# One-hot destination matrices made by comparing broadcast destination numbers instead of transposing, and a three-part pick done as one matrix product

## The chip, the cores and the metric

The kernel runs on one core of one Trainium2 chip. The metric is the device time of one execution in microseconds (us); a comparison of two kernels is by the median of several executions of each.

## What is computed

Eight blocks work one after the other on a matrix `x` of 1875 nodes by 256 features; each adds its result to `x`. Four are graph layers over the same 31,875 edges, which are sorted by destination (`dst`). The change touches two of the eight: it writes a table during the second block, and reads it in the third, the relational attention. The third block computes

```python
h_all = jnp.einsum('nf,rof->rno', x, W).reshape(r, n, h, d)      # r = 8 relations, h = 8 heads, d = 32
h_src, h_dst = h_all[edge_type, src], h_all[edge_type, dst]
scores = jnp.einsum('ehd,hd->eh', h_src, attn_src) + jnp.einsum('ehd,hd->eh', h_dst, attn_dst)
...                                                             # leaky relu, softmax over the edges of a destination
out = jax.ops.segment_sum(h_src * w[..., None], dst, num_segments=n)
```

and the second block lets the better half of the nodes, by a router weight, through a feed-forward network:

```python
weights = (jnp.einsum('bsd,do->bso', x, wr) + br)[..., 0]
_, idx = jax.lax.top_k(weights, k)
processed = jnp.zeros_like(x).at[batch_idx, idx[:, :kk]].set(y)  # y: the network's rows, times the weight
```

## The kernel before

**Tiling.** Nodes stand in T = 15 tiles of P = 128. Edges stand in EC = 264 chunks of 128, a chunk's edges all having their destination in one node tile; `g.dst[:, c]` holds for chunk c, one edge per partition, the destination's number within its tile (0 to 127), and a register `tiles[u]` says which tile. `g.dst`, `g.etype` and a large SBUF buffer `g.attrs_t` of [128, 264, 128] bf16 (the trace calls it `edge_space`) live through the whole program. Each phase (`Phase`) writes one program per engine by hand, with semaphores between them; the engines meet at a phase's end.

**The stage that the change rewrites** is `relation_rows` (phase `score`, 2376 to 2701 us in the profiled execution). It does two things side by side, in 22 passes of U = 12 chunks, each of 3 groups of G = 4 chunks.

- It makes the table `h_table` in DRAM, one node tile a pass in the first 15 passes ("product passes" below; the other 7 have none): ScalarE copies the tile of x to `x_tile` (L1965), TensorE makes four units of two relations each (`products`, L1924, two units before the picks and two behind them, in two PSUM buffers `p_rows`), ScalarE copies them to `rows` (L1974, L1977), and SyncE writes `rows`, 1,056 KB, to DRAM (L1898). `rows` is a single buffer: L1974 waits until the write has landed.
- It picks, for each edge, the destination's 64 attention numbers (8 relations x 8 heads) out of `score_dst`, by a product with a matrix that has a 1 where the edge's destination stands. VectorE compares `g.dst` with a row of numbers, once per chunk (`hot`, L1997), TensorE transposes the result (L1935), ScalarE copies it out of PSUM into `g.attrs_t` (L1969), and TensorE multiplies it by the numbers, which are held as three bf16 parts `parts[:, tile, k, :]` that sum to the f32 value: three matmuls of 64 columns per chunk, added up in PSUM (L1945). VectorE multiplies the sum by a 0/1 mask of the edge's relation (`rel`, made by L1991; L2004) and adds over the relations (L2008).

Beside these, GpSimd sends the scatters of a later block's adjacency matrix (`g.adj.send`, an indirect DMA of 128 values each, L488): two per group, once the group's comparisons are done (`hot_ready`), 132 in the stage. They are also sent in other phases, 45 of them in `rank`.

**The phases in the second block.** `rank_tokens` (phase `rank`, L1053 to L1109) computes a weight per node (L1080), writes the weights to DRAM and loads them back onto every partition (L1063, semaphore `w_spread`), and then counts with VectorE, in a loop over 15 tiles, how many nodes have a larger one (L1097 and its like). The DMA queue of ScalarE has nothing in it. `scatter_tokens` (phase `spread`) then sends the 15 tiles of rows with GpSimd (L1271) to their places; VectorE has nothing to do in it.

Of the kernel before, what the change touches and what calls it, by code (L numbers as in the profile page):

```python
# [13 lines left out]
P = 128  # L14
# [1025 lines left out]
def rank_tokens(nc, g, xn, wr, br, chosen, r):  # L1040
# [4 lines left out]
    with Phase(nc, "rank") as ph:  # L1045
# [5 lines left out]
        p_turned = ph.ps("p_turned", [T, P])  # L1051
        loaded, w_ready, w_turned, w_copied = (ph.sem(s) for s in ("loaded", "w_ready", "w_turned", "w_copied"))
# [16 lines left out]
        @block.tensor  # L1069
        def _(pe):  # L1070
            pe.wait_ge(w_ready, 1)
            nc.tensor.transpose(p_turned[:, :], w[:, :], g.ident[:, :]).then_inc(w_turned, 1)

# [187 lines left out]
def scatter_tokens(nc, g, rows, r, slots):  # L1261

    with Phase(nc, "spread") as ph:
# [4 lines left out]
        def _(pool):  # L1268
# [4 lines left out]
            pool.wait_ge(sent, 16 * r.choices * T)  # L1273

# [216 lines left out]
def capacity_ffn(nc, g, i):  # L1491

    chosen = max(max(1, int(0.5 * N)) - 1, 1)
    with Phase(nc, "cap") as ph:
# [7 lines left out]
        scatter_tokens(nc, g, xn, r, slots)  # L1502
# [359 lines left out]
def relation_rows(nc, g, score_src, score_dst, scores, xt, wt, h_table):  # L1862
# [4 lines left out]
    with Phase(nc, "score") as ph:  # L1867
        hot = ph.sb("hot", [P, U, P], BF16)
# [7 lines left out]
        rel, picked = ph.sb("rel", [P, U, R]), ph.sb("picked", [P, U, R, HD])  # L1876
        groups = U // G
        p_hot = [ph.ps(f"p_hot{b}", [P, G, P], BF16) for b in range(groups)]
        p_dst = [ph.ps(f"p_dst{b}", [P, G, 2 * S]) for b in range(groups)]
        turn, hot_ready, turned, copied = (ph.sem(x) for x in ("turn", "hot_ready", "turned", "copied"))  # L1880
# [4 lines left out]
        def _(sp):  # L1885

            sp.sem_inc(turned, groups)
            sp.sem_inc(copied, groups)
# [14 lines left out]
        def _(pool):  # L1903
            nc.gpsimd.iota(rel_idx[:, :], [[1, R]], base=0, channel_multiplier=0,
                           allow_small_or_imprecise_dtypes=True).then_inc(iota_made, 1)
            for n in range(EC // G):
                pool.wait_ge(hot_ready, n + 1)
                g.adj.send(pool, 2)

        @block.tensor  # L1910
        def _(pe):
# [47 lines left out]
        def _(act):  # L1959
# [21 lines left out]
            with act.Fori(T, EC // U) as i:  # L1981
                one_pass(i, False)
# [510 lines left out]
```

## Time and profile before

| what | value |
|---|---|
| median of 3 executions | 4655.58 us (4652.52 to 4660.18) |
| the profiled execution | 4685.71 us, its span 4684.1 us |
| busy over the span: TensorE, VectorE, GpSimd, ScalarE | 62%, 47%, 40%, 19% |
| `relation_rows` (phase `score`) | 2376 to 2701 us |
| its 15 product passes, its 7 others | 2387 to about 2613, to 2701 us |
| `rank` after the weights are back, until its end | 2119.1 to 2163.4 us |
| `spread` of the second block: first and last send | 2166.3, 2184.2 us |

The busy shares are means over eight blocks with different limits; what the change is worth is to be read in the stages it touches. The span is from the first to the last recorded instruction; the profiled execution is 30.1 us longer than the median of the three others.

### The profile page before, as it was taken

The numbers are of one execution on the slowest core, as the hardware profiler recorded it, in microseconds if no ns is written. First come the engines' busy times: TensorE is split into PE (matmuls) and PEld (weight loads), VectorE is DVE, ScalarE is ACT, GpSimd is POOL, SyncE is SP. The second block draws the span as 40 slices with busy tenths as digits, with TensorE's granted clock in tenths as the row PEclk, the third lists the DMA queues.
The fourth block names the chain that finished last, engine by engine and source line by source line (L and its number), as shares of the span: only waits on it lengthen the run. The fifth ranks groups of instructions, "written<-read, shape, count | busy, mean of one in ns | idle before, by whom it ended". The sixth has DMA issues, their size and how long they took to land. (4 is left out here: it accounts for less than half of the span.)

```text
span 4684.1 us, 57224 instructions
## 1 busy us (share of the span) xinstructions
PE 2923.7 (62%) x16851; PEld 2401.0 (51%) x16852; DVE 2212.2 (47%) x5663; ACT 867.9 (19%) x2228; POOL 1871.3 (40%) x1982
## 2 busy tenths in 40 slices
PE   3566746664666566642568626665949639947392
PEld 3455535553555355522556413335938639936382
DVE  6655645554555555564243437681064421134113
ACT  1122312221222122210112100001300103310020
POOL 4366546664666466624323467731010020020212
PEclk7788878777887778875678657676979859978696
DMA  6633323332333233303312133315947449945594
GB/s 157 217 89 89 78 65 89 88 83 59 89 90 88 57 87 89 89 15 124 100 55 74 28 82 93 92 41 190 304 145 240 150 159 328 325 150 174 181 333 128
DMA packets 357397, 598.97 MB, mean 128 GB/s; under 512 B 81862, under 2 KB 239864, under 8 KB 354808
## 3 DMA queue, kind: packets, MB, share of 16 engines
q1 hardware_dynamic: 245816, 357.76, 23.3%
q0 software_dynamic: 88640, 214.25, 16.3%
q10 hardware_dynamic: 22656, 23.54, 1.5%
q8 instruction: 132, 2.16, 0.2%
q14 instruction: 153, 1.25, 0.1%
HBM read 499.63 MB, written 95.75 MB: 127 GB/s over the span
## 5 line engine op out<-in xcount | busy, mean ns | idle before, releaser
L833 POOL DMA_INDIRECT gine_got<-gine_table,src x1056 | 1024.5, 970 | 619.7 <-issue 251.1
L893 PE MATMUL gine_p_sum<-gine_hot,gine_got 128*128 128x128 f32 x4224 | 846.2, 334 | 565.1 <-DVE stack_acc L930 200.1
L893 PEld LDWEIGHTS gine_p_sum<-gine_hot,gine_got 128*128 128x128 f32 x4224 | 707.4, 238 | 719.0 <-issue 648.6
L922 DVE TENSOR_TENSOR gine_got<-gine_got,gine_p_edge 128x256 f32<-128x256 f32 x1056 | 440.2, 418 | 633.5 <-PE gine_p_edge L884 365.0
L901 ACT ACTIVATE gine_got<-gine_got 128x256 f32<-128x256 f32 x1056 | 439.0, 417 | 1201.1 <-issue 750.5
L488 POOL DMA_INDIRECT adjacency<-value,place x264 | 281.1, 1065 | 475.9 <-POOLq L54 166.2
L930 DVE TENSOR_TENSOR stack_acc<-stack_acc,gine_p_sum 128x256 f32 x1056 | 438.9, 416 | 3.5 <-issue 0.7
L883 PE MATMUL gine_p_edge<-gine_w_a,edge_space 128*128 128x256 bf16 x1056 | 338.3, 320 | 42.6 <-issue 34.7
L1368 PE MATMUL ffn_p_h<-ffn_xt,ffn_w 128*128 128x128 f32 x2864 | 347.3, 279 | 1.1 <-DMA ffn_w<-in_L_ffn_w 0.7
L1368 PEld LDWEIGHTS ffn_p_h<-ffn_xt,ffn_w 128*128 128x128 f32 x2864 | 337.3, 196 | 3.8 <-DMA ffn_w<-in_L_ffn_w 2.6
L884 PE MATMUL gine_p_edge<-gine_w_b,edge_space 128*128 128x256 bf16 x1056 | 336.8, 319 | 0.0
L1380 PE MATMUL ffn_p_y<-ffn_w,ffn_ht 128*128 128x256 f32 x1432 | 328.8, 380 | 4.7 <-DMA ffn_w<-in_L_ffn_w 3.9
L2224 POOL DMA_INDIRECT edge_space<-h_table,hrow x264 | 273.8, 1037 | 123.0 <-issue 74.6
L2259 PE MATMUL inorder_p_sum<-edge_space,inorder_hot 128*128 128x265 f32 x528 | 230.9, 553 | 145.2 <-DVE edge_space L2332 95.9
L1434 DVE TENSOR_TENSOR ffn_y<-ffn_p_y,ffn_b 128x256 f32<-128x256 f32 x112 | 47.6, 425 | 549.4 <-PE ffn_p_y L1380 549.4
L1405 ACT ACTIVATE ffn_ht<-ffn_p_h,ffn_b 128x128 f32<-128x128 f32 x716 | 204.8, 368 | 548.3 <-PE ffn_p_h L1368 548.3
L1633 PE MATMUL gcn_p_out<-gcn_h,gcn_a 128*128 128x256 f32 x1350 | 298.7, 379 | 0.0
L1380 PEld LDWEIGHTS ffn_p_y<-ffn_w,ffn_ht 128*128 128x128 f32 x1432 | 263.6, 190 | 38.3 <-DMA ffn_w<-in_L_ffn_w 6.7
L1633 PEld LDWEIGHTS gcn_p_out<-gcn_h,gcn_a 128*128 128x128 f32 x1350 | 253.8, 190 | 32.9
L2259 PEld LDWEIGHTS inorder_p_sum<-edge_space,inorder_hot 128*128 128x128 f32 x528 | 110.8, 252 | 236.6 <-issue 230.0
L1146 POOL IOTA route_e_idx<- 128x8 f32 (+1 forms) x3 | 0.4, 135 | 570.2 <-POOLq L54 570.2
L844 DVE TENSOR_TENSOR gine_hot<-iota_free,dst 128x512 f32<-128x512 f32 x264 | 182.6, 692 | 66.1 <-PE gine_p_sum L893 33.0
(398 smaller groups left out, 3526.2 us busy)
## 6 DMA issues: line engine op xcount, KB each, us to landing
gcn_a<-adjacency SPq DMA_DIRECT2D x270, 320.0 KB
ffn_w<-in_L_ffn_W SPq DMA_DIRECT2D x74, 1024.0 KB
ffn_w<-in_L_ffn_w SPq DMA_DIRECT2D x60, 1024.0 KB
ffn_w<-in_L_ffn_w SPq DMA_DIRECT2D x90, 512.0 KB
adjacency<-zero_row ACTq DMA_DIRECT2D x3, 7200.0 KB, 43.8
gine_got<-gine_table,src POOLq DMA_INDIRECT x1056
h_table<-score_rows SPq DMA_DIRECT2D x15, 1056.0 KB
adjacency<-zero_row SPq DMA_DIRECT2D x1, 7200.0 KB, 28.1
```

The lines of the kernel that those rows point to most:

```text
L488: pool.indirect_dma_start(self.tables[c % 2], bass.IndirectOffsetOnAxis(ap=self.place[:, c:c + 1], axis=0), self.value[:, c:c + 1], None). ...
L833: pool.indirect_dma_start(got[:, c % RING, :], None, table, bass.IndirectOffsetOnAxis(ap=rows[:, c:c + 1], axis=0)).then_inc(gathered[c % ...
L883: nc.tensor.matmul(p_edge[c % 4][:, 0:D], g.attrs_t[:, c, :], w_a[:, :], start=True, stop=False)
L884: nc.tensor.matmul(p_edge[c % 4][:, 0:D], g.attrs_t[:, c, :], w_b[:, :], start=False, stop=True).then_inc(edge_done, 1)
L893: ins = nc.tensor.matmul(p_sum[d % 4][:, half * P:(half + 1) * P], got[:, d % RING, half * P:(half + 1) * P], hot[:, d % HOTS, :], start=T ...
L901: nc.scalar.activation(got[:, c % RING, :], got[:, c % RING, :], ACT.Relu).then_inc(msg_ready, 1)
L922: nc.vector.tensor_tensor(got[:, c % RING, :], got[:, c % RING, :], p_edge[c % 4][:, 0:D], ALU.add).then_inc(summed, 1)
L930: nc.vector.tensor_tensor(a, a, p_sum[d % 4][:, 0:D], ALU.add).then_inc(added, 1)
L1368: ins = nc.tensor.matmul(p_h[n % 2][m // 4][:, m % 4, :], w1_sb[:, n % 2, k, m * P:(m + 1) * P], xt[:, n % 2, k, :], start=(k == 0), stop= ...
L1380: ins = nc.tensor.matmul(p_y[n % 2][:, 0:D], ht[:, n % 2, m, :], w2_sb[:, n % 2, m, :], start=(m == 0), stop=(m == m_all - 1))
L1633: ins = nc.tensor.matmul(p_out[d][:, 0:D], a[:, n % RA, d * P:(d + 1) * P], h[:, t, :], start=(t == 0), stop=(t == T - 1))
L2259: nc.tensor.matmul(p_sum[c % SUMS][:, 0:WIDE], hot[:, c % HOTS, :], got[:, c % HELD, :], start=True, stop=True).then_inc(agg_done, 1)
```

## The change

A table of the destination numbers is made once, in `rank_tokens`: TensorE transposes `g.dst` (three pieces of 88 chunks), ScalarE copies them as bf16 and writes them to DRAM (`dst_lines`), and, once `w_spread` has come, issues three DMAs that bring the whole list onto every partition of `g.attrs_t` (3 x 128 x 22,528 bytes, 2.88 MB each). In `scatter_tokens` VectorE compares the buffer with the partition's own number, in place, in three instructions of 11,264 columns: that gives the turned 0/1 matrices of all 264 chunks. `relation_rows` loses the comparisons, the transposes and the copies; TensorE multiplies each chunk by all three parts at once (one matmul of 192 columns), and VectorE adds the three parts up, from PSUM, before it multiplies by the mask. GpSimd's two scatters per group now wait for the group's picks (`dst_done`).

```diff
@@ rank_tokens
+        K = 3
+        lines, lane_rows = g.dram("dst_lines", [EC * P], BF16), ph.sb("lane_rows", [EC // K, K, P], BF16)
+            for k in range(K):
+                ins = nc.tensor.transpose(p_lanes[:, k, :], g.dst[:, k * (EC // K):(k + 1) * (EC // K)], g.ident[:, :])
+            ins.then_inc(lanes_turned, 1)
             pe.wait_ge(w_ready, 1)
...
+        @block.scalar
+        def _(act):
+            act.wait_ge(lanes_turned, 1)
+            nc.scalar.copy(lane_rows[:, :, :], p_lanes[:, :, :]).then_inc(lanes_copied, 1)
+            act.wait_ge(lanes_copied, 1)
+            act.dma_start(lines.rearrange("(k c e) -> c k e", k=K, e=P), lane_rows[:, :, :]).then_inc(lanes_written, 16)
+            act.wait_ge(lanes_written, 16)
+            act.wait_ge(w_spread, 16)
+            for k in range(K):
+                some = slice(k * (EC // K), (k + 1) * (EC // K))
+                act.dma_start(g.attrs_t[:, some, :].rearrange("p c e -> p (c e)"), row(lines[some.start * P:some.stop * P]))\
+                    .then_inc(g.lanes_in, 16)
@@ scatter_tokens
+        @block.vector
+        def _(v):
+            if not mark_lanes:
+                return
+            v.wait_ge(g.lanes_in, 48)
+            for k in range(0, EC, EC // 3):
+                some = g.attrs_t[:, k:k + EC // 3, :]
+                nc.vector.tensor_scalar(some, some, g.iota_part[:, 0:1], None, ALU.is_equal)
@@ relation_rows
-        hot = ph.sb("hot", [P, U, P], BF16)
-        p_hot = [ph.ps(f"p_hot{b}", [P, G, P], BF16) for b in range(groups)]
-        p_dst = [ph.ps(f"p_dst{b}", [P, G, 2 * S]) for b in range(groups)]
+        p_dst = ph.ps("p_dst", [P, U // 2, 512])
...
             for n in range(EC // G):
-                pool.wait_ge(hot_ready, n + 1)
+                pool.wait_ge(dst_done, n + 1)
                 g.adj.send(pool, 2)
...
-                for b in range(groups):
-                    pe.wait_ge(hot_ready, i * groups + (b + 1))
-                    pe.wait_ge(copied, i * groups + (b + 1))
-                    for u in range(b * G, (b + 1) * G):
-                        ins = nc.tensor.transpose(p_hot[b][:, u % G, :], hot[:, u, :], g.ident_b[:, :])
-                    ins.then_inc(turned, 1)
...
                     pe.wait_ge(picked_done, i * groups + (b + 1))
-                    pe.wait_ge(copied, i * groups + (b + 1 + groups))
                     for u in range(b * G, (b + 1) * G):
-                        for k in range(3):
-                            ins = nc.tensor.matmul(p_dst[b][:, u % G, 0:S],
-                                                   g.attrs_t[:, bass.ds(i * U + u, 1), :].rearrange("p a e -> p (a e)"),
-                                                   parts[:, bass.ds(tiles[u], 1), k, :].rearrange("p a s -> p (a s)"),
-                                                   start=(k == 0), stop=(k == 2))
+                        ins = nc.tensor.matmul(p_dst[:, u // 2, u % 2 * 3 * S:(u % 2 + 1) * 3 * S],
+                                               g.attrs_t[:, bass.ds(i * U + u, 1), :].rearrange("p a e -> p (a e)"),
+                                               parts[:, bass.ds(tiles[u], 1), :, :].rearrange("p a k s -> p (a k s)"),
+                                               start=True, stop=True)
...
-                for b in range(groups):
-                    act.wait_ge(turned, i * groups + (b + 1 + groups))
-                    act.sem_inc(turn, 1)
-                    nc.scalar.copy(g.attrs_t[:, bass.ds(i * U + b * G, G), :], p_hot[b][:, :, :]).then_inc(copied, 1)
...
-                    v.wait_ge(turned, i * groups + (b + 1))
-                    for u in range(b * G, (b + 1) * G):
-                        ins = nc.vector.tensor_scalar(hot[:, u, :], g.iota_free[:, :], g.dst[:, bass.ds(i * U + u, 1)], None,
-                                                      ALU.is_equal)
-                    ins.then_inc(hot_ready, 1)
-                for b in range(groups):
...
                     v.wait_ge(dst_done, i * groups + (b + 1))
-                    nc.vector.tensor_tensor(picked[:, some, :, :], p_dst[b][:, :, 0:S].rearrange("p u (r h) -> p u r h", r=R),
-                                            rel[:, some, :].unsqueeze(3).to_broadcast([P, G, R, HD]),
-                                            ALU.mult).then_inc(picked_done, 1)
+                    nc.vector.tensor_reduce(summed[:, some, :].rearrange("p (a u) s -> p a u s", u=2),
+                                            p_dst[:, banks, 0:6 * S].rearrange("p a (u k s) -> p a u s k", u=2, k=3),
+                                            AX.X, ALU.add).then_inc(picked_done, 1)
+                    v.drain()
+                    nc.vector.tensor_tensor(picked[:, some, :, :], summed[:, some, :].rearrange("p u (r h) -> p u r h", r=R),
+                                            rel[:, some, :].unsqueeze(3).to_broadcast([P, G, R, HD]), ALU.mult)
                     v.drain()
                     nc.vector.tensor_reduce(scores[:, bass.ds(i * U + b * G, G), :], picked[:, some, :, :].rearrange("p u r h -> p u h r"),
                                             AX.X, ALU.add)
```

On TensorE the body of a product pass began before as follows (`ISA` and `REGISTER_ALU` rows are address arithmetic; the last row shown stands 36 times in a pass, each with an `ISA`):

```order
L793 ISA x2
L1935 MATMUL score_p_hot<-ident_b,score_hot 128x128 x4
...
L1931 REGISTER_ALU
L1935 MATMUL score_p_hot<-ident_b,score_hot 128x128 x4
L1919 REGISTER_ALU
L1921 ISA
L1924 MATMUL score_p_rows<-score_wt,score_x_tile 128x256 x4
L1921 REGISTER_ALU
L1924 MATMUL score_p_rows<-score_wt,score_x_tile 128x256 x4
L1942 REGISTER_ALU
L1945 ISA
L1945 MATMUL score_p_dst<-score_parts,edge_space 128x64
```

The same place now:

```order
L793 ISA x2
L1947 ISA
L1950 MATMUL score_p_rows<-score_wt,score_x_tile 128x256 x4
L1947 REGISTER_ALU
L1950 MATMUL score_p_rows<-score_wt,score_x_tile 128x256 x4
L1960 ISA
L1962 ISA
L1962 MATMUL score_p_dst<-score_parts,edge_space 128x192
```

The products are now the first thing in a pass, and the last row shown stands 12 times in a pass.

On VectorE a group's work stood after all 12 comparisons of its pass:

```order
L1997 TENSOR_SCALAR score_hot<-iota_free,dst 128x128
L1997 ISA
L1997 TENSOR_SCALAR score_hot<-iota_free,dst 128x128
L2004 TENSOR_TENSOR score_picked<-score_p_dst,score_rel 128x256
L2008 ISA
L2008 TENSOR_REDUCE rgat_scores<-score_picked 128x32
```

The same place now, with the first rows of the pass:

```order
L2002 TENSOR_TENSOR score_rel<-score_rel_idx,etype 128x96
L2007 ISA
L2008 TENSOR_REDUCE score_summed<-score_p_dst 128x256
L2012 TENSOR_TENSOR score_picked<-score_summed,score_rel 128x256
L2015 ISA
L2015 TENSOR_REDUCE rgat_scores<-score_picked 128x32
```

The comparisons are gone; each group has three instructions in place of two, and of them only the first reads PSUM. The multiplication L2012 now has both operands in SBUF.

## Rows read from the trace of the kernel before

**Rows 1.** Windows: awaiting `rank_every`, product passes, other passes.

```profile
core 0: us, PE busy (x) PEld busy (x) DVE busy (x) ACT busy (x) POOL busy (x), PEclk, DMA share, GB/s
2114.90:2119.20 4.30, 0.00 (x0) 0.00 (x0) 0.07 (x2) 0.00 (x0) 3.38 (x4) 0.50 0.67 229
2387.00:2613.00 226.00, 199.83 (x1206) 157.39 (x1207) 86.57 (x285) 63.21 (x134) 86.42 (x90) 0.84 0.25 67
2613.00:2701.00 88.00, 50.96 (x334) 32.31 (x331) 37.64 (x120) 12.54 (x22) 38.73 (x40) 0.53 0.04 13
```

**Rows 2.** Timeline of VectorE: starts of passes 2, 16 and 22.

```profile
2399.36 0.26 DVE L1991 TENSOR_TENSOR score_rel<-score_rel_idx,etype 128x96 f32<-128x96 f32 x1 [0.47 <-issue]
...
2609.24 0.26 DVE L1991 TENSOR_TENSOR score_rel<-score_rel_idx,etype 128x96 f32<-128x96 f32 x1 [0.45 <-issue]
...
2688.35 0.26 DVE L1991 TENSOR_TENSOR score_rel<-score_rel_idx,etype 128x96 f32<-128x96 f32 x1 [0.45 <-issue]
```

**Rows 3.** Timeline (start, us, engine ... [idle before <-releaser]), product pass.

```profile
2567.27 0.33 SPq L1898 DMA_DIRECT2D h_table<-score_rows  x1
2567.48 3.72 PE L1924 MATMUL score_p_rows<-score_wt,score_x_tile 128*128 128x256 f32 x16
...
2571.03 1.05 PE L1945 MATMUL score_p_dst<-score_parts,edge_space 128*128 x20
2572.04 0.24 ACT L1974 COPY score_rows<-rgat_in_score_src 128x64 f32 x1 [3.24 <-DMA h_table<-score_rows]
2572.23 0.97 POOL L488 DMA_INDIRECT adjacency<-value,place  x1 [0.30 <-issue]
...
2574.73 0.42 DVE L2004 TENSOR_TENSOR score_picked<-score_p_dst,score_rel 128x256 f32<-128x256 f32 x1 [7.58 <-PE score_p_dst L1945]
```

**Rows 4.** Timeline, the next product pass: `h_table` write, its landing.

```profile
2583.32 0.33 SPq L1898 DMA_DIRECT2D h_table<-score_rows  x1
...
2592.29 0.24 ACT L1974 COPY score_rows<-rgat_in_score_src 128x64 f32 x1 [7.43 <-DMA h_table<-score_rows]
```

**Rows 5.** Timeline of a pass without products.

```profile
2639.81 3.69 PE L1945 MATMUL score_p_dst<-score_parts,edge_space 128*128 x22
...
2644.43 0.96 POOL L488 DMA_INDIRECT adjacency<-value,place  x1 [0.30 <-issue]
...
2645.25 0.42 DVE L2004 TENSOR_TENSOR score_picked<-score_p_dst,score_rel 128x256 f32<-128x256 f32 x1 [5.89 <-PE score_p_dst L1945]
```

**Rows 6.** VectorE by line and shape: busy us, mean ns | idle before.

```profile
L2008 DVE TENSOR_REDUCE rgat_scores<-score_picked 128x256 f32 x66 | 40.4, 612 | 12.1 <-issue 12.1
L586 DVE TENSOR_REDUCE pairs_total<-pairs_p_sum 128x88 f32<-128x264 f32 x3 | 1.3, 426 | 0.0
L2004 DVE TENSOR_TENSOR score_picked<-score_p_dst,score_rel 128x256 f32<-128x256 f32 x66 | 28.0, 425 | 170.3 <-PE score_p_dst L1945 109.0 <-DMA unpack_rows<-in_edge_rows 59.3
```

**Rows 7.** The same view: a cast and a copy to bf16.

```profile
L440 DVE CAST unpack_parts<-unpack_rows 128x768 bf16<-128x768 f32 x11 | 6.2, 563 | 18.5 <-DMA unpack_rows<-in_edge_rows 18.5
L910 DVE COPY gine_w_a<-gine_parts 32x256 bf16<-32x256 bf16 x16 | 4.1, 257 | 0.5
```

**Rows 8.** Timeline of `rank`: a VectorE operation and a send.

```profile
2103.17 4.16 DVE L1080 TENSOR_TENSOR rank_prod<-cap_xn,rank_wr 128x3840 f32<-128x3840 f32 x1 [2.63 <-DMA rank_br<-in_L_ffn_br]
2103.28 4.90 POOL L488 DMA_INDIRECT adjacency<-value,place  x1 [0.30 <-issue]
```

**Rows 9.** Instructions of L1271: duration min/median/max, first and last start.

```profile
L1271 POOL DMA_INDIRECT cap_slots<-cap_xn,cap_slot x15: 965/971/973, 2166.3 to 2184.2; - x15
```

**Rows 10.** Timeline of `rank`: weights' load, ranking's first and last instruction.

```profile
2114.58 0.33 SPq L1063 DMA_DIRECT2D rank_every<-router_weights  x1
...
2119.13 2.21 DVE L1097 TENSOR_SCALAR_CACHE_REDUCE rank_junk<-rank_every,rank_w 128x1920 f32<-128x1920 f32 x1 [6.05 <-issue]
...
2163.21 0.17 DVE L1109 SCALAR_TENSOR_TENSOR cap_gate<-rank_rank,rank_w 128x15 f32<-128x15 f32 x1
```

More of the change, by code:

```diff
@@ L1051, in rank_tokens @@
         p_turned = ph.ps("p_turned", [T, P])
+        K = 3
+        lines, lane_rows = g.dram("dst_lines", [EC * P], BF16), ph.sb("lane_rows", [EC // K, K, P], BF16)
+        p_lanes = ph.ps("p_lanes", [EC // K, K, P])
+        lanes_turned, lanes_copied, lanes_written = (ph.sem(s) for s in ("lanes_turned", "lanes_copied", "lanes_written"))
         loaded, w_ready, w_turned, w_copied = (ph.sem(s) for s in ("loaded", "w_ready", "w_turned", "w_copied"))
@@ L1258, in _, with scatter_tokens @@
             nc.vector.tensor_scalar(r.expert[:, :], owner[:, :], float(ne - 1), None, ALU.min)
-def scatter_tokens(nc, g, rows, r, slots):
+def scatter_tokens(nc, g, rows, r, slots, mark_lanes=False):
     with Phase(nc, "spread") as ph:
@@ L1501, in capacity_ffn @@
         rank_tokens(nc, g, xn, i["L0_ffn_wr"].rearrange("d o -> (d o)"), i["L0_ffn_br"], chosen, r)
-        scatter_tokens(nc, g, xn, r, slots)
+        scatter_tokens(nc, g, xn, r, slots, mark_lanes=True)
         expert_blocks(nc, g, slots, results, r, i["L0_ffn_w1"].rearrange("(a d) f -> a d f", a=1), i["L0_ffn_b1"],
@@ L1875, in relation_rows @@
         rel_idx = ph.sb("rel_idx", [P, R])
-        rel, picked = ph.sb("rel", [P, U, R]), ph.sb("picked", [P, U, R, HD])
+        rel, picked, summed = ph.sb("rel", [P, U, R]), ph.sb("picked", [P, U, R, HD]), ph.sb("summed", [P, U, S])
         groups = U // G
-        p_hot = [ph.ps(f"p_hot{b}", [P, G, P], BF16) for b in range(groups)]
-        p_dst = [ph.ps(f"p_dst{b}", [P, G, 2 * S]) for b in range(groups)]
-        turn, hot_ready, turned, copied = (ph.sem(x) for x in ("turn", "hot_ready", "turned", "copied"))
+        p_dst = ph.ps("p_dst", [P, U // 2, 512])
+        turn = ph.sem("turn")
         split, dst_done, picked_done, iota_made = (ph.sem(x) for x in ("split", "dst_done", "picked_done", "iota_made"))
@@ L1885, in _ @@
         def _(sp):
-            sp.sem_inc(turned, groups)
-            sp.sem_inc(copied, groups)
             sp.sem_inc(picked_done, groups)
@@ L1980, in _ @@
                 one_pass(i, True)
-            with act.Fori(T, EC // U) as i:
-                one_pass(i, False)
         @block.vector
@@ L1993, in _ @@
                 for b in range(groups):
-                    v.wait_ge(turned, i * groups + (b + 1))
-                    for u in range(b * G, (b + 1) * G):
-                        ins = nc.vector.tensor_scalar(hot[:, u, :], g.iota_free[:, :], g.dst[:, bass.ds(i * U + u, 1)], None,
-                                                      ALU.is_equal)
-                    ins.then_inc(hot_ready, 1)
-                for b in range(groups):
-                    some = slice(b * G, (b + 1) * G)
-                    v.wait_ge(dst_done, i * groups + (b + 1))
-                    nc.vector.tensor_tensor(picked[:, some, :, :], p_dst[b][:, :, 0:S].rearrange("p u (r h) -> p u r h", r=R),
-                                            rel[:, some, :].unsqueeze(3).to_broadcast([P, G, R, HD]),
-                                            ALU.mult).then_inc(picked_done, 1)
+                    some, banks = slice(b * G, (b + 1) * G), slice(b * G // 2, (b + 1) * G // 2)
+                    v.wait_ge(dst_done, i * groups + (b + 1))
+                    nc.vector.tensor_reduce(summed[:, some, :].rearrange("p (a u) s -> p a u s", u=2),
[4 more added lines that the diff above has]
+                                            rel[:, some, :].unsqueeze(3).to_broadcast([P, G, R, HD]), ALU.mult)
                     v.drain()
@@ L2009, in _ @@
                                             AX.X, ALU.add)
-                    v.drain()
+                v.drain()
 def edge_scores(nc, g, h_table, scores):
@@ L2452, in build @@
         g.tile_of = sb("tile_of", [P, EC])
+        g.lanes_in = nc.alloc_semaphore("lanes_in")
         g.adj = Adjacency(nc, g, sb)
```

## The prediction

> **What bounds the kernel now.** I read the windows first, because the change lives in three places only: `rank` and `spread` of the second block, and the stage `relation_rows`. In the 15 product passes TensorE is busy 199.8 of 226 us, at a mean granted clock of 0.84; in the other passes 51.0 of 88 us, at 0.53, with VectorE at 37.6 us and GpSimd at 38.7 us [rows 1]. So no engine is full, and a busy share does not say what a pass costs. The starts of passes do: (2609.24 - 2399.36)/14 = 14.99 us for a product pass, (2688.35 - 2609.24)/6 = 13.19 us for another [rows 2]. All of the stage that the change can reach is 15 x 14.99 + 7 x 13.19 = 317 us.
>
> The timeline then shows what ends the waits in a product pass [rows 3]. Two halves of products cost 3.72 us each. The first group's 12 picks are over some 0.6 us after 2571.03 (20 take 1.05 us), but VectorE begins only at 2574.73, 1.53 us after the last of GpSimd's six sends ends (2572.23 + 0.97 = 2573.20). The pass without products shows it again: a third of 36 picks at 22 in 3.69 us would be done by 2641.8, and VectorE begins at 2645.25, in the last send [rows 5]. TensorE's finished work seems to be held while the sends run; the trace does not say why, and the sixth send is what I count from. The second limit is the table: written from 2567.27, landed at 2572.04, 4.8 us [rows 3]; the next takes 9.0 us (2583.32 to 2592.29) [rows 4]. Four passes of 15 have such a long one, the rest 4.3 to 5.0 us.
>
> **The change part by part.**
>
> *The stage, by its limits.* TensorE in a product pass: 1.06 us between passes, 3.72 + 3.72 for products, and 12 picks of 192 columns. One of 64 columns costs 1.05/20 = 0.052 us [rows 3], so between 12 x 0.052 = 0.6 us if width were free and three times that, 1.9; taken near the upper, 1.5. Sum 10.0.
>
> The table chain: the write 5.0 us, then ScalarE's copies 0.95, two units 3.72, a last copy 0.6: 10.3 us, and with the long write of rows 4 14.5; the mean over 11 and 4 is 11.4. The change takes nothing from this chain but the copies that stood beside it.
>
> VectorE: a group costs the new reduction R, then 0.425 for the product, 0.18 between, 0.61 for the second reduction and 0.24 of drains, 1.45 together [rows 6]; a pass has three groups and 0.8 for the mask. R adds 768 numbers up to 256 from PSUM, an operation that the trace lacks in this size. L586 (264 numbers from PSUM) takes 0.426; with a fixed 0.15 (L1109 takes 0.17 for 15 numbers [rows 10]) that is 1.05 ns per number, R = 0.95. L2008 takes 0.612 for 256 numbers read with a stride, 1.80 ns per number, R = 1.53. If L2008's extra 0.185 us is a price per output (32 outputs, 5.8 ns each), 256 outputs add 1.48 to 0.95: R = 2.43. The new one strides through its input as L2008 does, so I take 1.53: 3 x (1.53 + 1.45) + 0.8 = 9.7 us a pass, with 8.0 and 12.4 as ends. The picks wait for R of the group before in time (`picked_done`), and TensorE's other work hides that.
>
> GpSimd: six sends at 0.97 + 0.30 [rows 3] are 7.6 us, and now wait for the picks rather than for the comparisons. Behind each pair nothing is queued but the next pair; who suffers is the holding above. If it goes on, the last send ends 1.06 + 3.72 + 0.5 + 7.6 = 12.9 us after a pass's start, and with 1.5 a pass is 14.4 us. If it does not, the table's 11.4 stands. The hold is there in most product passes of the trace, so two parts to one: 13.4 us. **15 x (14.99 - 13.4) = 24 us saved.** In the other passes VectorE's 9.7 is the limit, plus some waiting on sends: 10.5. **7 x (13.19 - 10.5) = 19 us saved.** What the comparisons, transposes and ScalarE's copies cost lies in those passes already and is not counted again.
>
> *`rank`.* Transposes, a copy and a 68 KB write fit before `w_spread` (2119.1). Then 3 x 2.88 = 8.65 MB go onto 128 partitions. The load of `rank_every` moved 229 GB/s [rows 1], which makes 38 us; they land by 2119.1 + 38 = 2157, before VectorE's ranking ends at 2163.2 [rows 10]. Nothing else is on ScalarE's queue, and VectorE waits for `lanes_in` after the ranking only. Cost 0; without that cover up to 38 us.
>
> *`spread`.* Three comparisons of 11,264 columns in place, beside 15 sends from 2166.3 on [rows 9]. L910's 0.257 us for 256 bf16 numbers, less the fixed 0.15, is 0.42 ns each: 4.9 us a comparison. L440's 0.563 for 768 (from f32) gives 0.54 ns and 6.2 us [rows 7]. Beside a 4.16 us VectorE operation a send took 4.90 us in place of 0.97 [rows 8]: sends stand still while such an operation runs. Fully held the phase grows by 3 x 4.9 = 14 to 18 us; not at all, if sends slip between, 0. The first may start before a send is out, so I take 10.
>
> The Trainium skill (page "SBUF — State Buffer", section "SBUF: two separate sides") says that a VectorE operation in a two-port mode, or with two SBUF inputs against a GpSimd operation that reads SBUF, holds the port pair that the two share, and that GpSimd can then write no descriptors; the trace agrees with 4.90 beside 4.16 us [rows 8]. The page "VectorE: DVE Perf Modes" (section "The perf-mode tier table (the rule you actually need)") gives 693 ns for 2048 bf16 columns of such an operation; an estimate from it is 3.1 us a comparison, 9 us for three, and the sum would be better by 1 us or so.
>
> *Sum.* -24 - 19 + 10 = -33 us on the profiled 4685.7. That execution is 30 us over the median of 4655.6, and part of the holds may be due to its recording, so I take 10 off: -23, 4633 us.
>
> **The rivals.**
>
> *R1, the forecast*, chance 0.41: held in part, 4633, own range 4605 to 4655.
>
> *R2, the holds vanish*, 0.18. The sends now start in step with VectorE's reduction and are spread over a pass; for it speaks that the hold was seen where six sends ran in a row, against it that six in a row still follow the first picks, if picks are quick. Passes 11.4 and 9.7: -54 - 24 + 10 = -68, 4588 us.
>
> *R3, the reduction is dear*, 0.17. R = 2.43 makes VectorE's pass 12.4. For it: 256 outputs of three inputs each, which L2008 (eight each) and L586 price differently [rows 6]. Product passes 13.9, others 12.8: -16 - 3 + 10 = -9, 4647 us.
>
> *R4, slower: the new product waits on the sends*, 0.12. L2012 has both operands in SBUF, L2004 had one in PSUM, and the send released by the same `dst_done` reads SBUF just then. If each group's product waits for one send (0.97 us) and R is 2.43, VectorE's pass is 12.4 + 3 = 15.4: 15 x 0.4 + 7 x 2.2 + 10 = +31, 4687 us. It decides once VectorE's pass is over 15.0 us, and in the seven others from 13.2. Rows 8 show the block in the other direction; no row shows a VectorE operation waiting for a send. The skill's rule above would let whichever starts first block the other, which is this rival.
>
> *R5, the change does not do what it says*, 0.12: product passes stay at 15.0, set by hold and table write, and the others gain 0.7: -5 + 10 = +5, 4661 us.
>
> **How the numbers follow.** The time is R1's. From 4582 to 4668 lie R1, R3, R5 and most of R2; outside are R4 and the low tail of R2, 2 in 10 together. A measurement of this kernel tells about 0.2% (9.3 us) from no change. Faster by more than that: R1 but 0.05, R2, and half of R3, 0.63; slower: R4 and 0.04 of R5, 0.16; within: the rest, 0.21.
>
> **What would show it right or wrong.** Pass starts (now at L2002) 13.4 us apart with products, 10.5 without; L2008 at 1.5 us (0.95 and 2.4 are the others' values); L2012 at 0.43 or, by R4, over 1 us; L2008 idle before it "PE score_p_dst" long after the picks' end, if the hold stays; the last broadcast landed before 2163, and the sends of `spread` ending near 2195 in place of 2185. The prediction falls if `lanes_in` comes after the ranking, if other phases move by more than 5 us, or if the comparisons take over 7 us each.

## The result, and the profile after

The median went from 4655.0 us (4652.5 to 4660.2) to 4587.7 us (4581.3 to 4589.7), a ratio of 0.9851 with an interval of 0.9837 to 0.9866: 67 us faster, three times the forecast of 23 us and within 1 us of what the rival "the holds vanish" gave. One execution of e9_all_moved, 5759 us where its three others took 4304 to 4308, is left out of all times below.

The starts of passes 2, 16 and 22 in the changed kernel's timeline of VectorE:

```profile
2384.97 0.26 DVE L2002 TENSOR_TENSOR score_rel<-score_rel_idx,etype 128x96 f32<-128x96 f32 x1 [0.47 <-issue]
...
2539.46 0.26 DVE L2002 TENSOR_TENSOR score_rel<-score_rel_idx,etype 128x96 f32<-128x96 f32 x1 [0.45 <-issue]
...
2589.08 0.26 DVE L2002 TENSOR_TENSOR score_rel<-score_rel_idx,etype 128x96 f32<-128x96 f32 x1 [0.45 <-issue]
```

A product pass takes (2539.46 - 2384.97)/14 = 11.03 us where it took 14.99, another pass (2589.08 - 2539.46)/6 = 8.27 where it took 13.19 [rows 2]. That is 14 x 3.96 + 6 x 4.92 = 85 us of the profiled execution; the whole stage is 88 us shorter. The same two stretches as windows:

```profile
core 0: us, PE busy (x) PEld busy (x) DVE busy (x) ACT busy (x) POOL busy (x), PEclk, DMA share, GB/s
2384.97:2539.46 154.49, 122.77 (x605) 100.52 (x604) 84.84 (x141) 36.78 (x82) 81.28 (x85) 0.94 0.35 95
2539.46:2589.08 49.62, 21.02 (x87) 8.96 (x85) 36.07 (x60) 0.58 (x1) 33.41 (x35) 0.57 0.07 22
```

GpSimd's sends fill 81 us of 154 now, and VectorE 36 of 50 in the other passes. The granted clock rose from 0.84 in the product passes [rows 1] to 0.94. VectorE's instructions by line and shape (busy, mean ns):

```profile
L2008 DVE TENSOR_REDUCE score_summed<-score_p_dst 128x256 f32<-128x768 f32 x66 | 62.7, 950 | 71.4 <-PE score_p_dst L1962 68.8 <-issue 2.6
L2012 DVE TENSOR_TENSOR score_picked<-score_summed,score_rel 128x256 f32<-128x256 f32 x66 | 28.2, 427 | 6.1
```

The new reduction takes 0.95 us, the lower of the three values in the prediction, and the multiplication with two SBUF operands 0.427, as before with one in PSUM [rows 6]. All 66 of these lie between 0.424 and 0.478 us: none waits for a send of 0.97. A product pass in the timeline of all engines:

```profile
2412.65 1.15 PE L1962 MATMUL score_p_dst<-score_parts,edge_space 128*128 x12
2412.94 0.24 ACT L1987 COPY score_rows<-rgat_in_score_src 128x64 f32 x1 [3.98 <-DMA h_table<-score_rows]
...
2413.18 0.96 DVE L2008 TENSOR_REDUCE score_summed<-score_p_dst 128x256 f32<-128x768 f32 x1 [9.24 <-PE score_p_dst L1962]
2413.42 0.97 POOL L488 DMA_INDIRECT adjacency<-value,place  x1 [9.20 <-PE score_p_dst L1962]
...
2413.72 3.72 PE L1950 MATMUL score_p_rows<-score_wt,score_x_tile 128*128 128x256 f32 x16
...
2415.76 0.58 ACT L1990 COPY score_rows<-score_p_rows 128x512 f32<-128x512 f32 x1 [1.60 <-issue]
...
2417.48 0.58 ACT L1990 COPY score_rows<-score_p_rows 128x512 f32<-128x512 f32 x1 [1.14 <-PE score_p_rows L1950]
```

The reduction starts 0.5 us after the first pick, and the two copies 2.04 and 3.76 us after the products' start, while six sends run from 2413.42 on. These copies wait for products whose own records end 1.86 and 3.72 us after that start, so nothing holds them. Before, VectorE stood until 1.5 us behind the sixth [rows 3]. The hold on which the forecast counted is gone from the product passes, although the six sends still follow each other without a break there.

It, or something like it, remains elsewhere. Of the six other passes four take 7.2 us, one 8.8 and one 11.9. In the last of these TensorE's picks come 2.8 us apart, and VectorE stands until 3 us after the last of six sends (which ended at 2561.50):

```profile
2563.45 0.32 PE L1962 MATMUL score_p_dst<-score_parts,edge_space 128*128 x1 [2.47 <-issue]
...
2564.68 0.96 DVE L2008 TENSOR_REDUCE score_summed<-score_p_dst 128x256 f32<-128x768 f32 x1 [4.56 <-PE score_p_dst L1962]
```

That one pass is 0.8 us of the mean of 8.27.

Product passes are not alike either: of three, two take 9.2 to 9.5 us and one 13.9 to 16.6. In the long one the table write is long (timeline; its landing is what L1987 waits for):

```profile
2427.77 0.70 SPq L1924 DMA_DIRECT2D h_table<-score_rows  x1
...
2435.25 0.24 ACT L1987 COPY score_rows<-rgat_in_score_src 128x64 f32 x1 [7.41 <-DMA h_table<-score_rows]
```

7.5 us from issue to landing, 4.0 in the short passes (2408.90 to 2412.94).

What the change costs lies in `spread`. The comparisons as instructions of their line, and the first row send beside them in the timeline:

```profile
L1303 DVE TENSOR_SCALAR edge_space<-edge_space,iota_part x3: 3149/3149/3155, 2143.7 to 2149.9; 128x11264 bf16<-128x11264 bf16 x3
...
2144.34 5.73 POOL L1292 DMA_INDIRECT cap_slots<-cap_xn,cap_slot  x1 [4.62 <-PEq L54]
```

Three times 3.15 us. The first row send takes 5.73 us and the second 3.48, where one takes 0.97 [rows 9]. From the first to the last of the 15 it is now 25.1 us where it was 17.9 [rows 9]: 7.2 us lost, all in these two. `rank` is unchanged, 63.2 us from its multiplication to the first row send before and 63.3 now. The three transfers have landed some 20 us before the ranking ends. In a later profile (e15) they take 23.9 us, from 1890.0 to 1913.9, in place of the 38 of the prediction.

In the profiles the two kernels differ by 104 us, in the medians by 67. Some 22 us of that lie ahead of `rank` (its multiplication at 2103.2 and 2081.0), where the kernels are the same; four more profiles at that speed have 2082 to 2086, so the profiled execution of before was long there. The rest, 82 us, is 15 us more than the medians show.

### The profile page after: what moved, and what is told of

It reads as the page before. It is cut to its first block and busy times, and to the rows that moved or that the text cites. A ratio compares the mean times of both kernels' runs of the same rounds, so it can differ in the third digit from the quotient of the medians.

```text
span 4579.6 us, 54274 instructions
## 1 busy us (share of the span) xinstructions
PE 2819.1 (62%) x16062; PEld 2325.5 (51%) x16063; DVE 2228.5 (49%) x5468; ACT 832.3 (18%) x2163; POOL 1874.5 (41%) x1982
```

## The experiments

"Product pass" and "other" are the means over passes 2 to 15 and 16 to 21, from the starts of the instruction that makes the mask `rel`, as above. The chips differ: e1 to e4 ran on one (chip 10) where the kernel before takes 4654 us, the others on three (chips 0, 3 and 9) where it takes 4363 to 4367, most of the difference ahead of `rank`. The first comparison's chip is not on record; its kernel before took 4655 us, as on chip 10. "The slower chip" below is that of the 4654 and 4655 us. Each row has the time of the kernel before beside it, and ratios are to that. Runs with "no_sends", and e16, leave out half of the adjacency matrix's entries, so their result is incomplete.

| run | before, us | ratio (interval) | product pass | other |
|---|---|---|---|---|
| before / changed | 4655 | 1 / 0.985 (0.984 to 0.987) | 14.99 / 11.03 | 13.19 / 8.27 |
| e1_gate | 4654 | 1.003 (1.002 to 1.005) | 14.84 | 11.57 |
| e2_one_pick | 4654 | 1.007 (1.005 to 1.009) | 17.31 | 11.58 |
| e3_three_picks | 4654 | 1.001 (1.000 to 1.002) | 16.22 | 9.19 |
| e4_before_no_sends | 4654 | 0.989 (0.988 to 0.991) | 12.54 | 11.23 |
| e5_after_no_sends | 4365 | 0.981 (0.978 to 0.984) | 9.40 | 7.21 |
| e6_after_unrolled | 4365 | 0.989 (0.986 to 0.992) | 11.13 | 7.81 |
| e7_three_picks_no_sends | 4365 | 0.992 (0.989 to 0.995) | 12.30 | 8.12 |
| e8_sends_moved | 4365 | 0.989 (0.986 to 0.991) | 9.41 | 7.21 |
| e9_all_moved | 4367 | 0.986 (0.984 to 0.988) | 9.41 | 7.21 |
| e10_marks_moved | 4367 | 0.988 (0.986 to 0.990) | 10.89 | 7.28 |
| e11_pick_thrice | 4367 | 0.992 (0.990 to 0.994) | 11.69 | 7.24 |
| e12_thrice_no_sends | 4367 | 0.987 (0.986 to 0.989) | 11.23 | 7.23 |
| e13_narrow_apart | 4367 | 0.993 (0.992 to 0.995) | 12.30 | 7.89 |
| e14_wide_addresses | 4367 | 0.991 (0.990 to 0.993) | 11.72 | 7.23 |
| e15_after_again | 4367 | 0.989 (0.987 to 0.991) | 10.98 | 7.30 |
| e16_memset_for_sends | 4367 | 0.992 (0.990 to 0.995) | 12.54 | 8.09 |
| e17_before_again | 4363 | 1.001 (0.999 to 1.003) | 13.23 | 10.92 |
| e18_three_picks_again | 4363 | 0.996 (0.994 to 0.997) | 12.55 | 8.11 |

### One part of the change at a time

**e1_gate**: only the semaphore of the sends.

```diff
-                pool.wait_ge(hot_ready, n + 1)
+                pool.wait_ge(dst_done, n + 1)
```

> The kernel before with one line changed: GpSimd's two sends per group wait for the group's picks (dst_done) instead of its comparisons. Theories. A, many picks: TensorE's 36 picks of 64 columns per pass, each with address arithmetic, are what makes a product pass 15.0 us; B, sends: six sends in a row beside the first products hold TensorE's finished work; C, round trip: comparison, transpose, copy and pick stand one behind the other. By B product passes fall to about 11.5 us and the time to about 4600 us; by A and C it stays within 10 us of 4655, or is a little slower since the sends start later (up to 4680).

Product passes stayed at 14.8 us and the time rose by 0.3%, so theory B (the sends) failed in the form in which it was put. But the hold had only moved. From its timeline, in a stretch at full granted clock (1.00 from 2473.3 to 2488.0):

```profile
2480.79 3.71 PE L1924 MATMUL score_p_rows<-score_wt,score_x_tile 128*128 128x256 f32 x16
...
2484.67 1.02 POOL L488 DMA_INDIRECT adjacency<-value,place  x1 [0.30 <-issue]
2485.47 0.58 ACT L1977 COPY score_rows<-score_p_rows 128x512 f32<-128x512 f32 x1 [6.43 <-issue]
...
2487.03 0.58 ACT L1977 COPY score_rows<-score_p_rows 128x512 f32<-128x512 f32 x1 [0.98 <-DMA unpack_rows<-in_edge_rows]
```

The picks, now ahead of the sends, reach VectorE at once; the products behind them do not reach ScalarE at 2482.7 and 2484.5, as their records would have it, but at 2485.5 and 2487.0, the second 1.3 us behind the last send. In the passes without products nothing is left to hold, and they fell to 11.6.

**e2_one_pick**: only the picks; comparisons, transposes and copies stay.

```diff
-                        for k in range(3):
-                            ... p_dst[b][:, u % G, 0:S], ..., parts[:, bass.ds(tiles[u], 1), k, :] ...
+                        ... p_dst[:, b % 2 * 2 + u % G // 2, ...], ..., parts[:, bass.ds(tiles[u], 1), :, :] ...
```

> The kernel before with the second part of the change alone: one product of 192 columns per chunk and the sum of three parts on VectorE; comparisons, transposes and copies stay. The transposes share two PSUM buffers in place of three, and the picks two in place of three. By A (many picks) product passes fall to 11.5 to 12.5 us, the others to 11, time about 4605; by C (round trip) and B (sends) it stays at 4645 to 4665, since VectorE has 3 x 0.53 us more to do.

Slower by 0.7%, which no theory had. All product passes but the first last 17.3 us, to within 0.2. TensorE waits 3.9 us in each for a picks' buffer that two groups share. The hold is there too: the first reading begins 1.2 to 1.4 us after the last of the six sends in each of the passes 2 to 15. In one of them:

```profile
2513.01 0.97 POOL L488 DMA_INDIRECT adjacency<-value,place  x1 [0.31 <-issue]
...
2515.18 0.96 DVE L2005 TENSOR_REDUCE score_picked<-score_p_dst 128x256 f32<-128x768 f32 x1 [7.26 <-DMA unpack_rows<-in_edge_rows]
```

The eight picks before it ended at 2512.66 by their records, and the granted clock was 1.00 from 2506.0 to 2517.5, so a halved clock is not what holds them. (The DMA that the row names as releaser, `unpack_rows`, was over some 2000 us before.) Passes 2 to 6 have 6.8 us at half clock and the later ones 3.4, and they last the same 17.3 us. So one wide pick is no gain without the rest; how much of the loss is the hold and how much the fewer buffers this run does not say.

**e3_three_picks**: the changed kernel with the old picks and the old reading of them.

```diff
-                        ins = nc.tensor.matmul(p_dst[:, u // 2, u % 2 * 3 * S:(u % 2 + 1) * 3 * S], ..., parts[..., :, :], start=True, stop=True)
+                        for k in range(3):
+                            ins = nc.tensor.matmul(p_dst[b][:, u % G, 0:S], ..., parts[..., k, :], start=(k == 0), stop=(k == 2))
```

> The changed kernel with the old picks: three products of 64 columns per chunk, summed in PSUM, on the ready matrices. By A (many picks) product passes go back to 14 us or more and the time to about 4635; by C (round trip) it stays at 4580 to 4595; by B (sends gated by the picks) the same as C.

This speaks for theory A, the many picks: with the matrices ready but 36 narrow picks the whole gain was gone, 16.2 us a product pass. So on this chip neither half of the change is worth anything by itself.

**e4_before_no_sends**: `g.adj.send` left out of the stage.

> The kernel before without the 132 scatters of the stage (the adjacency matrix lacks half of its entries). By B (sends hold TensorE's results) product passes fall to about 11.5 us and the others to 10: about 4595 us. By A or C alone they stay at 15.0 and 13.2: 4655 us, less what the sends cost elsewhere.

12.5 us in place of 15.0, and 11.2 in place of 13.2: 1.1% faster, 47 us, where theory B alone had 11.5, 10 and 59. The sends cost the kernel before that much, and the forecast had rightly read that they do. The product passes are of two kinds: six of 11.6 us, at a granted clock of 0.92 to 1.00, and eight of 13.2 to 13.3, at 0.89 to 0.91.

### The sends and the table write in the changed kernel

**e5_after_no_sends**: the same edit in the changed kernel.

> The changed kernel without the 132 scatters of the stage (the adjacency matrix lacks half of its entries). In its profile two of three product passes last 9.4 us and the third 14 to 16, since the table write takes 8 us in place of 4. Theory S, sends and quick writes together make the long writes: all product passes 9.4 us or so, 15 x 1.6 = 24 us less, about 4563 us, all writes 3.5 to 4 us. Theory W, the write itself stalls when the stage writes quickly: the long writes stay, within 8 us of 4587.

Theory S (sends and quick writes together make the long writes) held: every product pass 9.4 us, from 9.2 to 9.5, every table write as short as the short ones, the granted clock 1.00. Against the changed kernel on such a chip (e15, 4319 us) it is 31 us less, where 24 were expected. The window of its product passes:

```profile
2173.43:2305.09 131.66, 116.78 (x621) 96.57 (x619) 84.93 (x140) 37.36 (x83) 0.00 (x0) 1.00 0.27 115
```

9.4 is TensorE's own chain (1.06 + 3.72 + 1.15 + 3.72 = 9.65, less the overlap of picks and products), 7.2 VectorE's: 3 x (0.95 + 0.43 + 0.61 + 0.18) + 0.7.

**e8_sends_moved** sent them in the next block's feed-forward phase, seven per block of rows:

```diff
+                if ne == 8 and affine is None and g.adj.next < EC:
+                    g.adj.send(pool, 7)
                 pool.wait_ge(y_ready, n + 1)
```

> The changed kernel with the 132 scatters sent in the feed-forward phase of the next block, seven behind each other per block of rows, in place of this stage. If the holds come from their neighbourhood in this stage and GpSimd has room in the later phase, the time is that of the run without sends, about 4565 us; if they hold the later phase's results (7 x 1.27 = 9 us per block of some 10), up to 4600 us.

The stage did fall to 9.4 and 7.2, and the time stayed at that of the changed kernel: the other phase went from 148.2 to 172.6 us for its 22 results, 8.2 us a block, since 7 x 1.27 = 8.9 us of sends are more than the 7.06 that a block took. The expectation had "some 10" for the 7.06, which was not read from a row.

**e10_marks_moved** put the comparisons, in twelve pieces, beside the capacity network's matrix work, where VectorE waits.

```diff
+                if mark_lanes and n < 6:
+                    if n == 0:
+                        v.wait_ge(g.lanes_in, 48)
+                    for k in range(2 * n * 22, (2 * n + 2) * 22, 22):
+                        some = g.attrs_t[:, k:k + 22, :]
+                        nc.vector.tensor_scalar(some, some, g.iota_part[:, 0:1], None, ALU.is_equal)
```

> The changed kernel with the comparisons alone moved, in twelve pieces, beside the capacity network's matrix work. If their 9.3 us hold GpSimd's row sends in spread, as the trace says (25.2 us from the first to the last in place of 17.9), the time falls by 7 us; if the phase is set by something else, it stays. The stage itself stays at 11.0 and 8.3 us per pass.

`spread` went back to 17.8 us, and the median was 4310 against 4319 of the changed kernel, on chips with the same time for the kernel before: 9 us, with intervals that overlap.

**e9_all_moved** has both, with three and five sends per block.

> The changed kernel with both costs moved to where their engine waits: the comparisons of the table in twelve pieces beside the capacity network's matrix work (VectorE waits there), and all 132 scatters out of the stage: three per block of rows in the capacity network (24) and five per block in the next block's (108), since seven per block, 8.9 us, were over that phase's 7.06 us per block. Expected: the stage 204 us in place of 236, the sends of spread 18 us in place of 25, the two networks unchanged: 35 us under the changed kernel. If the sends slow the networks' TensorE by being beside it, half of that is lost.

The fastest version that computes everything: 4304 us, 0.986 of the kernel before against 0.989. The stage takes 204 us in place of 228 (e15), but the next block's network 164.5 in place of 148.2 though five sends (6.4 us) fit into its 7.06 us, so 16 of 24 us were paid back: worse than the expectation's second case. (Both versions with moved sends change a wait in a branch for edge orders that don't occur here; it would need care.)

### Whose hold is it

**e6_after_unrolled**:

```diff
-            with pe.Fori(0, T) as i:
+            with pe.Fori(0, T // 2) as j:
+                one_pass(2 * j, True)
+                one_pass(2 * j + 1, True)
+            with pe.Fori(T - 1, T) as i:
                 one_pass(i, True)
```

> The changed kernel with TensorE's loop over product passes unrolled by two: the same instructions executed, twice as many in the loop's body (about 260 in place of 130). Theory H1, a long loop body is what delays TensorE's results beside GpSimd's sends (the kernel before had some 250 in a body): product passes go up by 2 to 4 us, time 4615 to 4640. Theory H2, the length of the body is without effect, and the number of instructions executed in a pass counts: 4583 to 4592.

Theory H2: 11.13 us against 10.98 for the changed kernel on such a chip (e15), no effect.

**e7_three_picks_no_sends** closes the square.

> Three picks per chunk on the ready matrices, as in the run with three picks, and without the stage's 132 scatters. With one pick per chunk against three (12 and 36 per pass) and with and without sends this makes a square of four. If the sends are what makes 36 picks dear, this falls from 4664 to about 4590 us, and product passes from 16.2 to 11.5; if the picks are dear by themselves, it stays above 4640.

12.3 us. With three picks the sends would cost 3.9 us a pass (16.2 to 12.3), with one 1.6 (11.0 to 9.4). That looked settled, but the four corners of the square were not on one chip.

**e11_pick_thrice** and **e12_thrice_no_sends** (`for _ in range(3):` around the wide pick):

> The changed kernel with every pick issued three times over (36 products of 192 columns per pass, the same result), with the sends. Theory I: 36 picks with their weight loads and address arithmetic are what lets GpSimd's sends hold back TensorE's next products, whatever their width: the copies of the second half's products come 2.5 us late or more, product passes go to 15.5 to 17 us, time about 4670 on the chip of 4655 (ratio 1.00). Theory P: the old shape, 64 columns summed in PSUM, did it: the passes grow by TensorE's own work alone, 24 x 0.08 = 1.9 us and 0.1 us of issue each, to some 13.5 us.

> The same without the stage's 132 scatters (the adjacency matrix lacks half of its entries). By theory I product passes fall to about 12.5 us; the difference to the run with sends is then 3 us or more per product pass, against 1.6 with twelve picks. By theory P the difference is 1.6 us here too.

11.7 and 11.2: no hold, so theory I does not hold on this chip. The sends cost 0.5 us a pass here. Every third write is still long, but at 6.2 to 8.3 us somewhat shorter than the 7.1 to 9.6 of e15, and a pass of 11.2 us covers more of it.

**e13_narrow_apart**, **e14_wide_addresses** and **e16_memset_for_sends**:

```diff
+                        for k in range(3):                      # e13
+                            ins = nc.tensor.matmul(p_dst[:, u // 2, (u % 2 * 3 + k) * S:(u % 2 * 3 + k + 1) * S], ..., parts[..., k, :], start=True, stop=True)
+                        for k in (4, 8, 0):                     # e14
+                            ins = nc.tensor.matmul(..., parts[:, bass.ds(tiles[(u + k) % U], 1), :, :] ..., start=True, stop=True)
+                    nc.gpsimd.memset(left[:, :, :], 0.0)        # e16, twice a group, on the kernel of e7
```

> The changed kernel with three picks of 64 columns per chunk, each into columns of its own, so that nothing is summed in PSUM and VectorE works as in the changed kernel; sends as in the changed kernel. If the narrow picks or their address arithmetic make the hold, product passes last 14.5 to 17 us and the second unit's copy comes 1.3 us after the last send; if the sum in PSUM or VectorE's reading did it, 11.0 to 12.5 us.

> 36 wide picks of 192 columns per pass as in the run with every pick thrice, but each with an address of its own (two of the three read another chunk's tile and are overwritten), so that TensorE's sequencer has 36 address computations. If the arithmetic makes the hold, product passes last 15 us or more; if narrowness does, 11.5 to 12 us as in that run.

> Three narrow picks per chunk summed in PSUM, and in place of the stage's 132 scatters as many memsets of 128 x 960 numbers by GpSimd (some 1 us each, no transfer; the adjacency matrix lacks half of its entries). If GpSimd's being busy is what holds TensorE's results, product passes are 16.2 us as with the sends; if the transfers are, 12.3 us as without.

> The changed kernel itself, for its stage and its ratio on this chip: product passes 11.0 us, the stage 230 to 237 us, 60 to 70 us under the kernel before.

12.3, 11.7 and 12.5 us: none has the hold. Narrow picks cost 0.6 us a pass more than wide ones done thrice, and the granted clock is lower beside them: 0.93 over the product passes against 0.99. The memsets cost nothing that can be told apart: e7, which has neither sends nor memsets, has the same two kinds of pass, 11.6 and 13.3 us, with six long ones in place of eight. The changed kernel repeats its product passes (10.98), and its other passes, 7.30, have no held one among them. Yet it is only 48 us under the kernel before here, not the 60 to 70 expected.

**e17_before_again** and **e18_three_picks_again** put the question to the chip.

> The kernel before, profiled on another chip. If its picks make the hold with the sends, product passes last 15.0 us again and the first group's reading begins 1.5 us after the last send; if the hold belongs to the first chip, they last 12.3 to 13.5 us. The ratio is 1 by construction.

> Three picks of 64 columns summed in PSUM, with the sends, on this chip. If the sum in PSUM or VectorE's reading of it makes the hold (against the same picks into columns of their own, 12.3 us), product passes last 16.2 us again; if it belongs to the first chip, 12.3 us, and the time is 0.993 of the kernel before.

The kernel before, unchanged, on a chip where it takes 4363 us, in the timeline of its sixth pass:

```profile
2217.32 1.20 PE L1945 MATMUL score_p_dst<-score_parts,edge_space 128*128 x24
...
2217.87 0.42 DVE L2004 TENSOR_TENSOR score_picked<-score_p_dst,score_rel 128x256 f32<-128x256 f32 x1 [4.46 <-PE score_p_dst L1945]
2218.48 0.97 POOL L488 DMA_INDIRECT adjacency<-value,place  x1 [0.30 <-issue]
```

VectorE reads the first picks 0.55 us after they start, in the fifth of six sends. The code that waited until 1.5 us behind the last send on the slower chip [rows 3] does not wait here; its product passes last 13.2 us, and the three long ones (16.3 to 17.6) stand beside long table writes. Three picks (e18) take 12.55 us where they took 16.22. So the hold belongs to the slower chip together with the code, not to the picks alone. There it needs the sends (e4), and the product passes keep it when only one part of the change is made (e1, e2, e3).

This also limits what e6, e11, e13, e14 and e16 say. They ran on chips where even the kernel before has no hold, so they do not tell whether the length of the loop, the number of picks, their width, their addresses or GpSimd's being busy makes the hold on the slower chip.

## Why the prediction was wrong

- **Product passes, 13.4 us forecast, 11.0 measured.** The failed step is the weight "two parts to one" for the hold going on. It did go on with the gate alone (e1), with the wide picks alone (e2) and with ready matrices and old picks (e3); it left the product passes only with both parts changed, and the trace of before can't show that. The other branch of that sum, the table chain's 11.4 us, was near in size partly by luck. It was to be eleven passes of 10.3 us and four of 14.5; it was ten of 9.2 to 9.5 us and four of 13.9 to 16.6. The short ones were forecast too long by the write, taken as 5.0 us and measured at 4.0. The rows of before had not said 5.0 either: apart from four long ones they lie between 3.3 and 4.8 us, not "4.3 to 5.0".
- **Other passes, 10.5 us forecast, 8.3 measured.** The term that was off is R: 0.95 us, as L586 had it (1.05 ns per number), not 1.53 by L2008's stride. 3 x 0.58 = 1.7 us of the 2.2 us. The row on the same memory (PSUM) with the same count of three inputs was the nearer one. The rest of VectorE's pass was 0.7 us too long as well: undisturbed passes take 7.2 us, since no drains of 0.24 us a group come on top. The 0.8 us for waits on sends was nearly right in size (1.1 measured) and wrong in kind: it is mostly one held pass of six, not L2012, which takes 0.427 us. On the faster chip nothing of it is left (7.30 us).
- **`spread`, 10 us forecast, 7.2 measured**: right in mechanism, and a comparison took 3.15 us, not 4.9. The estimate from the Trainium skill's "VectorE: DVE Perf Modes" (section "The perf-mode tier table (the rule you actually need)") was 3.1 us, nearer than the one from my rows.
- **`rank`, 0 forecast**, 0.2 us measured; the broadcasts were covered as said, with more room than said (24 us in place of 38).
- **The rival on the other side** (L2012 waits on sends) did not happen: none of its 66 rows is longer than 0.478 us. The port rule of the Trainium skill's page "SBUF — State Buffer" (section "SBUF: two separate sides") agrees with the traces in the direction VectorE over GpSimd only (`spread`, a send of 5.73 us).
- **The rival "the holds vanish"** had 11.4 and 9.7 us and 4588 us, with a chance of 0.18. It is nearly what happened, but its number was met by luck. Its reason, sends spread over a pass, is not there: six sends still run in a row from 2413.42 on. Its other passes were 1.4 us too long and `spread` 3 us too dear, against the profiles, which show 15 us more gain than the medians do. And it lacked the 10 us that the forecast took off for the recording; with them it would have been 4598. On the faster chips the same change gives 48 us.

What stays open: what holds TensorE's results on the slower chip, and why both parts of the change are needed to free the product passes. TensorE's sequencer has address instructions of some 0.7 us there, among ones of 0.03 to 0.08: 37 over 0.3 us in the stage of before, 24 of them while sends run, and 29 and 19 in the changed kernel. There is none in the fourteen profiles of the faster chips, nor without the sends (e4). But e1 has 2, e2 none and e3 9, and they are slow all the same. The square of picks and sends was not completed on the slower chip, where e5 and e7 never ran.

## What to carry to other kernels

A wait that always ends at the same distance behind another engine's last instruction, whatever its own producer does, is worth an experiment before it is priced: leave that engine's work out. Profile the kernel before on a second chip too, and early: here 19 us of the gain are a chip's, and five experiments looked for a hold on chips that do not have it. Where a cost is bounded from two rows, take the one on the same memory and with the same inputs per output. Work moved beside another phase is free only while its time per step stays under that phase's, and even then (e9) not wholly.

## What the runs showed of the hardware

- A DMA write of 1,056 KB lands in 4.0 us, but every third one in 6.2 to 9.6 us when scatters of 128 single values run beside it and writes start 9.4 to 11.2 us after each other (the changed kernel, e11, e15; from the issue to the ScalarE copy that waits). In the kernel before, at 15 us a pass, four of 14 take 7.9 to 9.0. Without the scatters none of 14 writes takes over 4.2 us (e4, e5, e7, e12), and at 12 to 13 us a pass three of 14 are long (e13 up to 6.1 us, e17 up to 9.7).
- TensorE's 36 weight loads and products of 192 columns take 1.8 us more a pass than 12 (e12 against e5), at a granted clock of 1.00 in both. With 36 of 64 columns (e7) eight of 14 passes take 2.2 us more and six, at 0.89 to 0.91, 3.9 us.
- Two indirect sends beside VectorE's comparisons in place, 11,264 bf16 columns in 3.15 us each, took 5.73 and 3.48 us in place of 0.97 (`spread`). Beside sends a VectorE product of two SBUF operands kept its 0.42 to 0.48 us.
- The same kernel takes 4654 us on chip 10 and 4363 to 4367 on chips 0, 3 and 9; some 210 us of that lie ahead of `rank`. On the slower one TensorE's finished work reached VectorE only after the last of six indirect sends in most product passes, 1.4 to 1.8 us behind it in the kernel before and 1.2 to 1.4 in e2. On chip 3 it reached VectorE while they ran (e17).
